# One attention stage with float32 operands split into two float32r terms, its softmax in two pieces, its tokens loaded first

## The reference

```python
xn = layernorm(x)                       # over the 192 channels, eps 1e-5
q, k, v = xn @ Wq.T + bq, xn @ Wk.T + bk, xn @ Wv.T + bv
att = softmax(q @ k.T * 192 ** -0.5)    # 2304 queries x 2304 keys, one head of 192 channels
y = x + (att @ v) @ Wc.T + bc
```

## Time and profile before

| what | value |
|---|---|
| time, median of 3 runs | 7393.43 us (7389.38 to 7394.81) |
| span of the profiled execution, from first to last instruction | 7380.8 us |
| TensorE busy, whole span | 6377.0 us (86%) |
| VectorE busy, whole span | 4608.4 us (62%) |
| ScalarE busy, whole span | 3166.2 us (43%) |
| `wide_attention`, first issue to last store's issue | 2925.49 to 4330.25 us |

### The profile page before, as it was taken

The page is one execution under the profiler, slowest core; times in us unless marked ns, Lnnn a source line. Parts: engine busy times, 40 slices in busy tenths (PEclk is TensorE's granted clock), DMA queues, the critical chain, the costliest instruction groups (busy, mean ns, idle before and its releaser), DMA issues. The chain is left out here.

```text
span 7380.8 us, 232267 instructions
## 1 busy us (share of the span) xinstructions
PE 6377.0 (86%) x87259; PEld 4216.1 (57%) x87259; DVE 4608.4 (62%) x7530; ACT 3166.2 (43%) x5364; POOL 2362.9 (32%) x2687
## 2 busy tenths in 40 slices
PE   6799999999986775799999981597889999999977
PEld 4366666666655552576776771365545555555546
DVE  6798889888953201232332345012779999999976
ACT  2077777777771241223222220122444444454432
POOL 0011112111210000000000001201279999999961
PEclk8699999999997886899999975798999999999986
DMA  4211111111115224101100022332821111111123
GB/s 118 83 39 40 39 40 46 43 39 40 41 39 141 78 60 133 30 1 29 30 1 20 1 73 76 77 76 72 256 90 37 37 38 37 36 38 37 37 68 106
DMA packets 424900, 428.39 MB, mean 58 GB/s; under 512 B 77729, under 2 KB 397961, under 8 KB 419051
## 3 DMA queue, kind: packets, MB, share of 16 engines
q1 hardware_dynamic: 342123, 339.77, 16.5%
q0 software_dynamic: 62528, 59.16, 3.4%
q10 hardware_dynamic: 19712, 21.53, 0.9%
HBM read 253.62 MB, written 166.55 MB: 57 GB/s over the span
## 5 line engine op out<-in xcount | busy, mean ns | idle before, releaser
L653 DVE TENSOR_REDUCE softmax_part_max<-softmax_ring 128x1 f32<-128x512 f32 (+1 forms) x2880 | 1624.1, 630 | 219.4 <-PE softmax_ring L560 161.5
L2540 POOL TENSOR_TENSOR retention_decayed<-retention_third,retention_decay_table 128x384 f32<-128x384 f32 x1728 | 1690.6, 1006 | 101.5 <-ACT retention_third L2562 97.0
L2521 DVE TENSOR_TENSOR retention_decayed<-retention_scores,retention_decay_table 128x768 f32<-128x768 f32 x1728 | 1650.9, 958 | 91.8 <-PE retention_scores L2482 60.9
L689 ACT ACTIVATE softmax_probs<-softmax_scores 128x768 f32<-128x768 f32 x1728 | 1393.5, 811 | 376.4 <-PE softmax_scores L584 267.0
L2482 PE MATMUL retention_scores<-retention_q_half,retention_k_piece 96*32 96x384 bf16 x20736 | 1185.7, 325 | 35.2 <-DMA retention_v_piece<-ret_v 28.8
L2562 ACT COPY retention_third<-retention_scores 128x384 f32<-128x384 f32 x1728 | 828.3, 479 | 888.4 <-PE retention_scores L2482 888.4
L2494 PE MATMUL retention_sums<-retention_decayed,retention_v_piece 128*32 128x288 f32 x13824 | 1183.6, 406 | 3.1 <-POOL retention_decayed L2540 0.6
L560 PE MATMUL softmax_ring<-softmax_k_next,softmax_q_next 96*32 96x512 bf16 (+1 forms) x11520 | 1115.8, 370 | 44.2 <-DMA softmax_k_next<-rope_k 31.7
L584 PE MATMUL softmax_scores<-softmax_q_third,softmax_k_piece 99*32 99x384 bf16 x13824 | 892.0, 328 | 61.4 <-ACT softmax_probs L689 28.5
L2482 PEld LDWEIGHTS retention_scores<-retention_q_half,retention_k_piece 96*32 96x32 bf16 x20736 | 626.8, 95 | 517.3 <-DVE retention_decayed L2521 46.6
L595 PE MATMUL softmax_sums<-softmax_probs,softmax_v_piece 128*32 128x192 f32 x13824 | 887.5, 328 | 12.4 <-ACT softmax_result L670 6.2
(11 more groups left out here) (304 smaller groups left out, 6672.0 us busy)
## 6 DMA issues: line engine op xcount, KB each, us to landing
ret_v<-ret_proj_values SPq DMA_DIRECT2D x8, 1728.0 KB, 8.7
retention_v_piece<-ret_v SPq DMA_DIRECT2D x144, 96.0 KB
softmax_q_third<-rope_q SPq DMA_DIRECT2D x192, 54.0 KB
softmax_q_next<-rope_q POOLq DMA_DIRECT2D x64, 162.0 KB, 4.1
softmax_k_piece<-rope_k SPq DMA_DIRECT2D x192, 54.0 KB
softmax_k_next<-rope_k POOLq DMA_DIRECT2D x64, 162.0 KB, 6.9
ret_q<-ret_proj_parts SPq DMA_DIRECT2D x48, 216.0 KB, 2.8
ret_k<-ret_proj_parts SPq DMA_DIRECT2D x48, 216.0 KB, 3.1
```

The lines of the kernel that those rows point to most:

```text
L653: nc.vector.reduce_max(part_max[:, j, c:c + 1], ring[m % DEEP][:, 0:CHUNKS[c][1]], axis=X)\
L689: nc.scalar.activation(probs[n % 4][:, :].rearrange("p (c q) -> p c q", c=2), scores[n % 2][:, :, 0:QC], ACT.Exp, scale=scale).then_inc(ex ...
L2521: nc.vector.tensor_tensor(weights[n % 4][:, 0:2 * QC].rearrange("p (c q) -> p c q", c=2), scores[n % 2][:, 0:2, 0:QC], table[:, table_at(n ...
L2540: nc.gpsimd.tensor_tensor(weights[n % 4][:, 2 * QC:HALF], third[n % 3][:, :], table[:, at:at + QC], ALU.mult)\
```

## The change

Queries, keys, values and transposed probabilities are kept as two float32r tensors each, a high term (ScalarE's copy, rounded to float32r) and a low term (VectorE subtracts the high term from the full value in the bank). Each product becomes three: high with high, high with low, low with high. For the values, high and low stand side by side in `v_terms`, so that one matmul of 384 columns makes two of the three, and one of 192 the third; the division by the sum then adds two halves. Each ring bank is now copied by ScalarE and subtracted by VectorE, one after the other, before it is free. Transposes, projections and output stay float32.

Maximum, exponential and sum are done in two pieces, of columns 0 to 1023 and 1024 to 2303; the exponentials need one buffer instead of two. TensorE waits for the second piece only at turn 2, and the value products wait group by group.

The tokens of image 0 are the first load of the stage. `normed` is raised after every three tiles, and the transposes take both channel halves of a group before the next group.

```diff
@@ LayerNorm
-        last.then_inc(self.normed, 1)
+            if t % self.TPC == self.TPC - 1:
+                last.then_inc(self.normed, 1)
     def transposes(self, pe, b):
-        pe.wait_ge(self.normed, b + 1)
         for g in range(2 * self.CHUNKS):
-            half, c = divmod(g, self.CHUNKS)
+            c, half = divmod(g, 2)
+            if half == 0:
+                pe.wait_ge(self.normed, b * self.CHUNKS + c + 1)
@@ wide_attention
-        qk_t = sb("qk_t", [P, 2, 2, N], F32)
-        v = sb("v", [P, TILES, C], F32)
-        probs = [sb(f"probs{i}", [P, N], F32) for i in range(2)]
-        probs_t = sb("probs_t", [P, N], F32)
+        qk_hi, qk_lo = (sb(f"qk_{n}", [P, 2, 2, N], F32R) for n in ("hi", "lo"))
+        v_terms = sb("v_terms", [P, TILES, 2, C], F32R)
+        probs = sb("probs", [P, N], F32)
+        probs_hi, probs_lo = (sb(f"probs_{n}", [P, N], F32R) for n in ("hi", "lo"))
...
+        EARLY = 1024
+        HALVES = [(0, EARLY), (EARLY, N)]
+        TERMS = [(qk_hi, qk_hi), (qk_hi, qk_lo), (qk_lo, qk_hi)]
@@ sync
+            ln.load(sp, 0, x[0, :, :], first=True)
             for to, of in [(identity[:, :], ident), (wv[:, :, :], w_v),
...
-            ln.load(sp, 0, x[0, :, :], first=True)
@@ tensor
             def long_part(i, c):
                 at, width = CHUNKS[c]
-                nc.tensor.matmul(scores[:, at:at + width], qk_t[:, 0, 0, i * P:(i + 1) * P], qk_t[:, 1, 0, at:at + width],
-                                 start=True, stop=False)
+                for k, (q, keys) in enumerate(TERMS):
+                    nc.tensor.matmul(scores[:, at:at + width], q[:, 0, 0, i * P:(i + 1) * P], keys[:, 1, 0, at:at + width],
+                                     start=(k == 0), stop=False)
             def short_parts(i):
...
+                for pair in (CHUNKS[0:2], CHUNKS[2:4], CHUNKS[4:]):
+                    for k, (q, keys) in enumerate(TERMS):
+                        for r, (at, width) in enumerate(pair):
+                            rows = slice(r * OVER, r * OVER + OVER)
+                            last = nc.tensor.matmul(scores[:, at:at + width], q[rows, 0, 1, i * P:(i + 1) * P],
+                                                    keys[rows, 1, 1, at:at + width], start=False, stop=(k == 2))
+                    if pair[0][0] != EARLY:
+                        last.then_inc(scored, 1)
             def turn(b, i, g):
-                pe.wait_ge(pt_act, (b * TILES + i) * len(ON_ACT) + (g // 2 if g % 2 == 0 else 0))
-                pe.wait_ge(pt_dve, (b * TILES + i) * len(ON_DVE) + (g // 2 if g % 2 else 0))
+                m = i * NG + g
+                pe.wait_ge(pt_lo, b * TURNS + max(m - 1, 0))
...
                 for t in range(TILES):
-                    last = nc.tensor.matmul(valued_bank[:, 0:C], probs_t[:, t * P:(t + 1) * P], v[:, t, :],
-                                            start=(t == 0), stop=(t == TILES - 1))
+                    if t % 4 == 0:
+                        pe.wait_ge(pt_lo, b * TURNS + i * NG + t // 4 + 1)
+                    keys = slice(t * P, (t + 1) * P)
+                    nc.tensor.matmul(valued_bank[:, 0:2 * C], probs_hi[:, keys], v_terms[:, t, :, :].rearrange("p s c -> p (s c)"),
+                                     start=(t == 0), stop=False)
+                    last = nc.tensor.matmul(valued_bank[:, 0:C], probs_lo[:, keys], v_terms[:, t, 0, :],
+                                            start=False, stop=(t == TILES - 1))
@@ scalar
+                    for k, (at, to) in enumerate(HALVES):
+                        nc.scalar.activation(probs[:, at:to], scores[:, at:to], ACT.Exp, bias=shift[:, i % 2:i % 2 + 1],
+                                             scale=scale, accum_out=total[:, i % 2, k:k + 1]).then_inc(exped, 1)
...
+                    for g, (t0, n) in enumerate(TGROUPS):
+                        m = i * NG + g
+                        act.wait_ge(pt_full, b * TURNS + m + 1)
+                        nc.scalar.copy(probs_hi[:, t0 * P:(t0 + n) * P], ring[m % 2][:, 0:n * P]).then_inc(pt_hi, 1)
@@ vector
+            def low_projections(b):
+                for n in range(USES):
+                    dve.wait_ge(proj_hi, b * USES + n + 1)
...
+                        nc.vector.tensor_tensor(qk_lo[:, i, half, part], bank(n)[:, 0:ln.W],
+                                                qk_hi[:, i, half, part].bitcast(F32), ALU.subtract).then_inc(proj_free, 1)
...
             def shifts(b, i):
+                for k, (at, to) in enumerate(HALVES):
+                    dve.wait_ge(scored, (b * TILES + i) * 2 + k + 1)
+                    nc.vector.reduce_max(top[:, i % 2, k:k + 1], scores[:, at:to], axis=X)
...
             def copies(b, i):
+                    dve.wait_ge(pt_hi, b * TURNS + m + 1)
+                    part = slice(t0 * P, (t0 + n) * P)
+                    nc.vector.tensor_tensor(probs_lo[:, part], ring[m % 2][:, 0:n * P], probs_hi[:, part].bitcast(F32), ALU.subtract)\
+                      .then_inc(pt_lo, 1)
             def take_values(b, i):
...
+                nc.vector.tensor_tensor(whole[:, s], total[:, i % 2, 0:1], total[:, i % 2, 1:2], ALU.add)
+                dve.drain()
+                nc.vector.reciprocal(inverse[:, s], whole[:, s])
+                dve.drain()
+                nc.vector.tensor_scalar(heads[:, i, :], valued_bank[:, C:2 * C], inverse[:, s], None, ALU.mult)
+                dve.drain()
+                nc.vector.scalar_tensor_tensor(heads[:, i, :], valued_bank[:, 0:C], inverse[:, s], heads[:, i, :], ALU.mult, ALU.add)\
+                  .then_inc(scaled, 1)
             def image(b, with_next):
+                low_projections(b)
                 dve.wait_ge(out_full, b * OUTS)
```

More of the change, by code:

```diff
@@ L3 @@
 from contextlib import ExitStack
-F32, BF16, I32 = mybir.dt.float32, mybir.dt.bfloat16, mybir.dt.int32
+F32, F32R, BF16, I32 = mybir.dt.float32, mybir.dt.float32r, mybir.dt.bfloat16, mybir.dt.int32
 ALU = mybir.AluOpType
@@ L1338, in wide_attention @@
         NG = len(TGROUPS)
-        ON_ACT = [g for g in range(NG) if g % 2 == 0]
-        ON_DVE = [g for g in range(NG) if g % 2]
+        TURNS = TILES * NG
+        EARLY = 1024
+        HALVES = [(0, EARLY), (EARLY, N)]
+        TERMS = [(qk_hi, qk_hi), (qk_hi, qk_lo), (qk_lo, qk_hi)]
         OUTS = 2 * (TILES // 3)
@@ L1403, in long_part @@
                 at, width = CHUNKS[c]
-                nc.tensor.matmul(scores[:, at:at + width], qk_t[:, 0, 0, i * P:(i + 1) * P], qk_t[:, 1, 0, at:at + width],
-                                 start=True, stop=False)
+                for k, (q, keys) in enumerate(TERMS):
+                    nc.tensor.matmul(scores[:, at:at + width], q[:, 0, 0, i * P:(i + 1) * P], keys[:, 1, 0, at:at + width],
+                                     start=(k == 0), stop=False)
             def short_parts(i):
-                for c, (at, width) in enumerate(CHUNKS):
-                    rows = slice(c % 2 * OVER, c % 2 * OVER + OVER)
-                    last = nc.tensor.matmul(scores[:, at:at + width], qk_t[rows, 0, 1, i * P:(i + 1) * P],
-                                            qk_t[rows, 1, 1, at:at + width], start=False, stop=True)
@@ L1412, in short_parts @@
-                last.then_inc(scored, 1)
+                for pair in (CHUNKS[0:2], CHUNKS[2:4], CHUNKS[4:]):
[6 more added lines that the diff above has]
+                        last.then_inc(scored, 1)
@@ L1513, in _ @@
         def _(dve):
+            def low_projections(b):
+                for n in range(USES):
+                    dve.wait_ge(proj_hi, b * USES + n + 1)
+                    if n < QK_USES:
+                        i, rest = divmod(n, 2 * ln.CHUNKS)
+                        half, c = divmod(rest, ln.CHUNKS)
+                        part = slice(c * ln.W, (c + 1) * ln.W)
+                        nc.vector.tensor_tensor(qk_lo[:, i, half, part], bank(n)[:, 0:ln.W],
+                                                qk_hi[:, i, half, part].bitcast(F32), ALU.subtract).then_inc(proj_free, 1)
+                    else:
+                        t = 2 * (n - QK_USES)
+                        nc.vector.tensor_tensor(v_terms[:, t:t + 2, 1, :], bank(n)[:, 0:2 * C].rearrange("p (t c) -> p t c", c=C),
+                                                v_terms[:, t:t + 2, 0, :].bitcast(F32), ALU.subtract).then_inc(proj_free, 1)
@@ L1514, in shifts @@
             def shifts(b, i):
-                dve.wait_ge(scored, b * TILES + i + 1)
-                nc.vector.reduce_max(top[:, i % 2:i % 2 + 1], scores[:, 0:N], axis=X)
+                for k, (at, to) in enumerate(HALVES):
+                    dve.wait_ge(scored, (b * TILES + i) * 2 + k + 1)
+                    nc.vector.reduce_max(top[:, i % 2, k:k + 1], scores[:, at:to], axis=X)
                 dve.drain()
-                nc.vector.tensor_scalar(shift[:, i % 2:i % 2 + 1], top[:, i % 2:i % 2 + 1], -scale, None, ALU.mult)\
-                  .then_inc(shifted, 1)
```

(5 more changed lines are left out.)

38 lines of the change are left out of this document (14 added, 24 removed).

## The result

The changed kernel takes **7285.49 us** (median of 4 runs, 7273.3 to 7292.89). The kernel before took 7394.12 in the same comparison; the ratio is 0.9852, 95% interval 0.984 to 0.9864: 108.6 us less. The forecast was 7250, 143 less. The direction and the mechanism held, and a quarter of the gain is missing.

What follows compares the result with a forecast made beforehand. TensorE was taken to set the pace (tile 14.23 to 12.68 us); 114 us less over four images and 28 at the start, 142 off 7393.4, gave 7251, rounded to 7250, range 7195 to 7330.

Steps and rivals of the forecast that it cites:

- The price of a float32r product: On TensorE, one cycle a column as in bfloat16: 0.216 us for 512 columns, 0.163 for 384.
- 4: float32r streams every column at two cycles: long 1.29, short 3.2, value 8.8, tile 20.3; 7800 us; chance 0.08.
- 3: Narrow value product costs what float32 costs, 0.33 us; tile 16.6, 7532 us, slower than before; chance 0.12.
- The floor: In short float32r products the next weights load behind the current stream; 192 or 256 columns take 0.112 us.
- the second case below: Case that float32r weight loads are accelerated, so the floor under short streams goes; no size given at that place.
- rival 1: No floor under short products: 192 columns at 0.080, short pairs at 0.216; tile 12.05, 7207 us; chance 0.20.
- The stall: At each tile's third turn TensorE waits for VectorE's subtraction of group 0's bank, 0.83 us.
- Softmax: Behind the value products: first exponential ends at 3.7 us, second at 5.1, needed at 7.3; one piece, 5.2, would show.
- Ends of an image: Per image: tile 0's open scores and softmax 3.5 us less, last tile 0.9 more, projections' last subtraction 0.6 more.
- Start: Tokens load first, constants land 2 to 4 us after issue; stage start 28 us less, bounds 20 to 31.
- The 12.6 us held fixed: Difference of the profiled span, 7380.8, from the median, 7393.4, kept unchanged in the forecast sum.
- 2: Narrow value product at half rate, 0.165 instead of 0.112 us, 0.95 a tile; 7318 us; chance 0.12.

Runs made afterwards that it cites:

- bfloat16 run: Terms kept as bfloat16 instead of float32r, same three products, against the changed kernel: 7192.78 us, ratio 0.9752.
- 128-column run: Second value product (low probabilities, high values) cut from 192 to 128 columns, against the changed kernel: 7268.35 us in a single run.

## Why the prediction was right, and where the 34 us are

| term | forecast | measured |
|---|---|---|
| tile: start to third turn | 2.36 | 2.23 (3080.07 to 3082.30) |
| third turn to short products | 3.49 | 3.69 (to 3085.99) |
| short products | 1.89 | 1.93 (to 3087.92) |
| value products | 4.94 | 5.20 (to 3093.12) |
| tile | 12.68 | 13.05 |
| an image's tiles, less | 26.4 | 21.2 |
| an image's ends, less | 2.0 | 1.4 |
| start, less | 28 | 24.2 |
| sum, less | 142 | 4 x 22.6 + 24.2 = 114.6 |

- *What bounds it.* Right: TensorE sets the pace before and after, at a clock of 0.99 to 1.00, after with one wait a tile.
- *The price of a float32r product.* The choice between the two ends was right (one record; half or full float32 price would have given rivals 4 and 3), the size was not: bfloat16's 0.42 ns a column from the earlier trace rows was taken, and float32r takes 0.451. That is 0.015 on each of the nine products of 512 columns in the second line, 0.14 of its 0.20; the rest lies behind the wait, where the third turn and its products take 1.19 and the next ones 1.14. The bfloat16 run has the forecast price to the nanosecond, 0.216. The Trainium skill, "FP8 and Floating Point Precision", TensorE Precision Notes, calls the reduced form a plain truncating read; the single record agrees, the 7% stands in no row of before.
- *The floor.* Right in kind: the 128-column run shows a floor, and with bfloat16's loads, half as long, it is gone. The pair was sized 0.163 + 0.112 and took 0.286; of the 0.011, 0.010 is the dearer column of the wide product. 18 x 0.011 is 0.20 of the 0.26 that the value products are over. The sign, records 0.163 and 0.112 apart, did not come as stated: they are 0.20 and 0.085 apart, the wait being ahead of the narrow record and not behind it. Where the text ties accelerated loads to "the second case below", its numbers are those of rival 1.
- *The stall.* Right in place, engine and reason; 0.83 forecast, 0.66 by starts. TensorE reaches it 0.04 later with the dearer products, and the subtraction lets it go 0.13 earlier: it begins at 1.50 in the tile (3081.57) and not behind the values at 1.60, while the last scaling still runs.
- *Softmax.* Maxima 1.225 and 1.481 against 1.23 and 1.49. In the tile shown the second exponential ends, its sum read, 4.7 us after the value products begin, 5.1 forecast: hidden. That it would show in one piece is right; what this would cost a tile was not priced, and it costs 0.07.
- *Ends of an image.* The open stretch fell from 13.27 to 10.0, 3.3 of the 3.5 forecast. An image's first tile fell from 16.3 to 13.95, more than the others. That is 0.8 an image more than the 1.55 forecast for every tile, and was luck: it hides some 3 us of the miss. Everything else of an image's end is 1.9 longer, 1.5 forecast.
- *GpSimd.* The term put at nothing is nothing: the 96 subtractions of queries and keys take 557 to 559 ns each, also beside the bias addition (2972.0 to 2982). The normalising operations, up to 4446 in the earlier trace rows, now take 371 to 384.
- *Start.* The step that failed is the landing: 2 to 4 us after the issue was taken for the constants, without a row for it; 7.7 measured, and 7.7 to 7.9 in five more kernels with this order. The tokens' side was right: normalised 24.3 us after the first issue, 27.5 forecast, well ahead.
- *The 12.6 us held fixed.* They are not time around the span: the changed kernel's profiled execution took 7286.52 with a span of 7285.0. The profiled execution before was a quick one. The term stands on both sides and changes no difference.
- *Rivals.* 1 falls by the 128-column run for float32r; in bfloat16 there is no floor. 2 and 3 fall by the pair's 0.286, which leaves 0.113 for the narrow product beside the wide one's 0.173, against 0.165 and 0.33; 4 falls by the 0.231 of the long products.

So of the missing 27.4 us of stage, 4 are the start's landing and 23 lie in the images. There the products are 0.50 a tile dearer than forecast, of which the dearer column makes up nearly 0.4 (the 0.14 and 0.20 above, and 0.04 in the short products); the earlier subtraction gives 0.13 back, and the first tile of an image and its ends shift the rest by small amounts both ways. The mechanism stood; the mis-sized term is the price of a float32r column, 0.451 ns for 0.42.

## What to carry to other kernels

Price an unseen data type by its own rows or leave its range wide on the dear side: here 7% a column makes up most of the fifth of the stage's gain that is missing. Where a copy is made a chain of two engines, look at the order of what feeds it first: a product moved between two turns gave back 40 us of the stage, more than twice the 15 to 19 of the two-piece softmax. And before an edit is blamed for a loss, read which stage lost it: 130 us appeared in code that nobody touched, in the execution that was profiled.

## What the runs showed of the hardware

- A float32r product with 128 weight columns is one record; successive ones start 0.231 us apart for 512 columns and 0.173 for 384 at a clock of 0.99 to 1.00, bfloat16 0.216 and 0.162.
- A pair of float32r products with 384 and with 192 or 128 moving columns takes 0.286 either way; in bfloat16 384 with 192 takes 0.245. A load of 128 x 128 weights lasts 188 to 191 ns (medians) in float32r, 190 in float32 and 98 in bfloat16.
- A loop's time can hang on its place in an engine's instruction list: retention 1744 to 1747 us with 12 packets of instructions in it, 1875 with 128 and 1911 with 165, and back with 18 idle instructions ahead.
- Three loads of 388 KB together took 20 us to issue on SyncE and 36 on ScalarE, and while they alone ran, the DMA engines moved some 20 GB/s (18 to 25 in the changed kernel, 2939 to 2959).
